# Deformable stages: transposes and hats first, pointwise sums in the taps' PSUM banks, first positions read one stage earlier

## What is computed

```python
def deform_block(x, ow, ob, dw, pw, pb, K):
    offsets = conv2d(x, ow, ob, K // 2)             # 2*K*K channels
    out = deform_depthwise(x, offsets, dw, K, K // 2)
    return conv2d(out, pw, pb, 0)                   # pointwise, 128 -> 128
...
# deform_depthwise: for each of K*K taps, sample x bilinearly at (gy+ky+dy, gx+kx+dx), times dw[tap], summed
out3 = deform_block(c3, ..., 3); out5 = deform_block(c5, ..., 5); out7 = deform_block(c7, ..., 7)
out = jnp.concatenate([out3, out5, out7], axis=1)
return out * se_weight(out, fc1_w, fc2_w)           # squeeze and excitation over mean and maximum
```

## Time and profile before

| | us |
|---|---|
| median of 3 runs (lowest, highest) | 7206.5 (7201.03, 7209.59) |
| the profiled execution, as timed | 7206.31 |
| its span, first to last instruction | 7204.5 |
| TensorE busy | 6456.0 (90%) |
| VectorE busy | 5057.3 (70%) |
| ScalarE busy | 4072.4 (57%) |
| GpSimd busy | 800.5 (11%) |
| mean granted TensorE clock, as a share of 2.4 GHz | 0.949 |

### The profile page before, as it was taken

One profiled execution on the slowest core, in us unless ns is written; L12 is line 12 of the kernel. 1 busy time (PEld: TensorE's weight loads), 2 busy tenths in 40 slices (PEclk: granted clock), 3 DMA queues, 4 the chain that ended last, 5 costly groups with the idle time before them and its releaser, 6 DMA issues. The chain is left out here.

```text
span 7204.5 us, 129062 instructions
## 1 busy us (share of the span) xinstructions
PE 6456.0 (90%) x48970; PEld 4356.8 (60%) x48970; DVE 5057.3 (70%) x10274; ACT 4072.4 (57%) x5674; POOL 800.5 (11%) x580
## 2 busy tenths in 40 slices
PE   6999999999998788998888988889888896999898
PEld 3555555555554455786557865578655785555598
DVE  6877877877877577887778877788777887233323
ACT  3655656656655255786557865578655785111132
POOL 3211211211211200201002010020100200000000
PEclk9999999999999899899998999989999898999899
DMA  3010000000000443554435544355443554010499
GB/s 114 16 33 24 16 33 24 16 33 24 17 33 20 118 114 90 130 116 112 110 91 133 115 113 108 85 136 118 115 100 89 132 122 123 27 44 35 108 224 207
DMA packets 182729, 616.12 MB, mean 86 GB/s; under 512 B 56553, under 2 KB 65185, under 8 KB 139347
## 3 DMA queue, kind: packets, MB, share of 16 engines
q1 hardware_dynamic: 182019, 606.89, 33.5%
HBM read 540.66 MB, written 65.59 MB: 84 GB/s over the span
## 5 line engine op out<-in xcount | busy, mean ns | idle before, releaser
L2288 PE MATMUL b_p<-m_S,b_hkt 64*128 64x144 f32 (+37 forms) x27520 | 2119.5, 309 | 300.1 <-DVE b_acc L2170 144.1
L2288 PEld LDWEIGHTS b_p<-m_S,b_hkt 64*128 64x128 f32 x27520 | 1970.2, 195 | 526.0 <-DVE m_S L2237 267.0
L2237 DVE TENSOR_TENSOR m_S<-m_rx,m_ry 128x140 f32<-128x140 f32 (+26 forms) x5312 | 1618.0, 357 | 359.2 <-PE b_p L2288 177.6
L2142 ACT ACTIVATE m_rx<-m_pp,b_mcol 128x512 f32<-128x512 f32 (+6 forms) x1328 | 764.9, 647 | 901.5 <-DVE m_S L2237 899.4
L539 ACT ACTIVATE a_ex<-a_p_t 128x1024 f32<-128x1024 f32 x526 | 539.0, 1025 | 719.1 <-PE a_p_t L471 717.1
L603 DVE TENSOR_REDUCE a_nm<-a_p_x 128x1 f16<-128x1024 f32 x537 | 658.3, 1226 | 279.1 <-PE a_p_x L460 262.0
L2146 ACT ACTIVATE m_ry<-m_pp,b_mrow 128x544 f32<-128x544 f32 (+6 forms) x1328 | 762.5, 645 | 0.0
L2170 DVE SCALAR_TENSOR_TENSOR b_acc<-b_p,b_dwc,b_acc 128x323 f32<-128x323 f32 (+14 forms) x1088 | 624.8, 577 | 189.9 <-PE b_p L2288 189.9
L1725 PE MATMUL b_p<-b_hp,b_ow 128*98 128x512 f32 x1568 | 732.4, 618 | 0.0
L609 DVE TENSOR_TENSOR a_el<-a_ex,a_eh 128x1024 f16<-128x1024 f32 x525 | 692.9, 1320 | 11.3 <-issue 7.7
L2178 DVE SCALAR_TENSOR_TENSOR b_acc<-b_p,b_dwc,b_acc 128x1024 f32<-128x1024 f32 x384 | 491.1, 1279 | 99.0 <-PE b_p L2288 97.6
(11 more groups left out here) (217 smaller groups left out, 6884.1 us busy)
## 6 DMA issues: line engine op xcount, KB each, us to landing
m_pp<-sampling_positions SPq DMA_DIRECT2D x664, 512.0 KB, 6.4
d_win<-merged_kernels SPq DMA_DIRECT2D x192, 263.0 KB, 6.8
b_xin<-x SPq DMA_DIRECT2D x24, 1024.0 KB, 8.4
a_xr<-in_x SPq DMA_DIRECT2D x12, 1536.0 KB, 6.4
a_xh<-in_x SPq DMA_DIRECT2D x9, 1536.0 KB, 6.4
x<-a_xr SPq DMA_DIRECT2D x9, 1536.0 KB, 5.8
c_xs<-x SPq DMA_DIRECT2D x9, 1536.0 KB, 6.3
b_xr<-x SPq DMA_DIRECT2D x13, 1024.0 KB, 14.1
```

Of the source, the lines that this page charges most:

```text
L2142: last = e.activation(rx[:, u, xo[c]:xo[c + 1]].rearrange("p (a b) -> p a b", a=H), pp[:, b, 1, :].rearrange("p (a b) -> p a b", a=H)[:, : ...
L2237: e.tensor_tensor(S[:, k % NS, 0:(r1 - r0) * w].rearrange("p (a b) -> p a b", b=w), rx[:, u, xo[cc]:xo[cc + 1]].rearrange("p (a b) -> p a ...
L2288: last = e.matmul(G[:, a0 - top:z0 - top, c0 - left:c1 - left], hkt[64 * s:64 * s + 64, SIDE * cr + cc, :], S[64 * s:64 * s + 64, k % NS, ...
```

## The change

- TensorE begins a stage with the transposes, and VectorE, not ScalarE, copies them to `hkt`. The four pointwise matmuls follow and write `ps[1]` and `ps[2]`, banks of the taps that the first part of tap 0 doesn't use, with no wait between them.
- ScalarE begins with the hats of tap 0, then evacuates the pointwise sums (`take_sums`), then goes on to tap 1. TensorE waits for these evacuations before the second and third part that it writes (j = 1, 2).
- SyncE reads the positions of a stage's tap 0 at the end of the stage in front, as soon as a ring slot is free, and waits there until they have landed; the slot is shifted by `RING_AT` so that it fits. For the first stage the setup block does it.
- For that the tiles `pp`, `rx`, `ry`, `S` and the setup's and `sample_far`'s tiles are cut from one room `work` that lives through the layer.

```diff
 FIRST_UNITS = 8
...
-        self.bank = [0, 1] * 4 + ([1] * SE_UNITS + [0] if g == 0 else [c % 2 for c in range(len(own))])
+        self.bank = [0, 1] * 2 + ([1] * SE_UNITS + [0] if g == 0 else [c % 2 for c in range(len(own))])
...
+        work = a.sb("work", [P, 16960])
+        pp, rx, ry, S = carve(work, [((NB, 2, N), F32), ((2, HAT), F32), ((2, HAT), F32), ((NS, WIDEST), F32)])
...
+        def read_positions(e, pp, g, tap, sem):
+            for s in range(2):
+                e.dma_start(pp[64 * s:64 * s + 64, (tap + RING_AT[g]) % NB, :, :], posd[g][s, 2 * tap:2 * tap + 2, :].partition_broadcast(64)).then_inc(sem.sem, 16)
...
+        def sums_in_taps(e, gp):
+
+            for i in range(4):
+                s, n = divmod(i, 2)
+                e.matmul(ps[1 + s][:, n, :], pw[:, gp, :], acc[:, s, n * HALF:(n + 1) * HALF], start=True, stop=True).then_inc(s_pw.sem, 1)
+
+        def take_sums(e, gp, stage):
+            for i in range(4):
+                s, n = divmod(i, 2)
+                e.wait_ge(s_pw.sem, s_pw.at(stage * 4 + i + 1))
+                e.sem_inc(sh["tick"], 1)
+                e.activation(dcv[:, gp, s, n * HALF:(n + 1) * HALF], ps[1 + s][:, n, :], ACT.Identity, bias=pb[:, gp:gp + 1],
+                             accum_out=sums[:, gp, s, n:n + 1]).then_inc(s_pe.sem, 1)
+
...
+                        for r in range(2):
+                            e.wait_ge(s_st[r].sem, s_st[r].at(FIRST_UNITS // 4 * 16))
+                        read_positions(e, pp, 0, 0, taps[0].s_pp[RING_AT[0]])
...
-                    pp = am.sb("pp", [P, NB, 2, N])
-                    rx = am.sb("rx", [P, 2, HAT])
-                    ry = am.sb("ry", [P, 2, HAT])
-                    S = am.sb("S", [P, NS, WIDEST])
...
-                            if tap < TAPS:
-                                b = tap % NB
+                            if 0 < tap < TAPS:
+                                b = (tap + RING_AT[g]) % NB
                                 if tap >= NB:
                                     e.wait_ge(tp.s_ab.sem, tp.s_ab.at(2 * (tap - NB + 1)))
-                                if tap == 1:
-                                    e.wait_ge(tp.s_pp[0].sem, tp.s_pp[0].at(32))
-                                for s in range(2):
-                                    e.dma_start(pp[64 * s:64 * s + 64, b, :, :], posd[g][s, 2 * tap:2 * tap + 2, :].partition_broadcast(64)).then_inc(tp.s_pp[b].sem, 16)
+                                read_positions(e, pp, g, tap, tp.s_pp[b])
                             if tap == 0 and g == 2:
...
+                        done = next(n for n in range(TAPS - NB, TAPS) if (n + RING_AT[g]) % NB == RING_AT[nxt])
+                        e.wait_ge(tp.s_ab.sem, tp.s_ab.at(2 * (done + 1)))
+                        ahead = taps[nxt].s_pp[RING_AT[nxt]]
+                        read_positions(e, pp, nxt, 0, ahead)
+                        e.wait_ge(ahead.sem, ahead.at(32))
...
-                        filled(e, us[7])
+                        filled(e, us[3])
...
-                        take_pointwise(e, gp, us[0:4])
-                        for j in range(4):
-                            u = us[4 + j]
-                            filled(e, u)
-                            part = bank_of(u[1]).rearrange("p (i c) -> p i c", c=P)
-                            e.activation(hkt[:, 4 * j:4 * j + 4, :], part, ACT.Copy, scale=-1.0 if j >= TURNED else 1.0).then_inc(s_cu[u[1]].sem, 1)
                         for tap in range(TAPS):
-                            u, b = tap % 2, tap % NB
+                            u, b = tap % 2, (tap + RING_AT[g]) % NB
                             (rows, yo), (cols, xo) = tap_spans(K, tap)
...
+                            if tap == 0:
+                                take_sums(e, gp, stage)
...
-                                    filled(e, us[3])
+                                    e.wait_ge(s_pw.sem, s_pw.at(stage * 4 + 4))
+                                    e.sem_inc(sh["tick"], 1)
...
-                                largest(e, gp, s, us)
+                                e.wait_ge(s_pe.sem, s_pe.at(stage * 4 + 2 * s + 2))
+                                e.sem_inc(sh["tick"], 1)
+                                largest(e, gp, s)
...
+                        for j in range(4):
+                            filled(e, us[j])
+                            part = bank_of(us[j][1]).rearrange("p (i c) -> p i c", c=P)
+                            e.tensor_scalar(hkt[:, 4 * j:4 * j + 4, :], part, -1.0 if j >= TURNED else 1.0, None, ALU.mult).then_inc(s_cu[us[j][1]].sem, 1)
                         if K in QUARTERED:
-                            filled(e, us[3])
+                            e.wait_ge(s_pw.sem, s_pw.at(stage * 4 + 4))
+                            e.sem_inc(sh["tick"], 1)
                             e.memset(acc[:], 0.0).then_inc(tp.s_g.sem, 1)
...
-                        pointwise(e, gp, us[0:4])
                         e.wait_ge(s_h8.sem, s_h8.at(pr * 3 + g + 1))
                         for j in range(4):
-                            free_bank(e, us[4 + j])
+                            free_bank(e, us[j])
                             for i in range(4):
-                                last = e.transpose(bank_of(us[4 + j][1])[:, i * P:(i + 1) * P], h8[:, 4 * j + i, :, :, :].rearrange("p s i j -> p (s i j)"), sh["ident"][:])
+                                last = e.transpose(bank_of(us[j][1])[:, i * P:(i + 1) * P], h8[:, 4 * j + i, :, :, :].rearrange("p s i j -> p (s i j)"), sh["ident"][:])
                             last.then_inc(s_pu.sem, 1)
+                        sums_in_taps(e, gp)
                         for c, k in plan.ahead:
                             convolve(c, k)
-                        for u in us[6:8]:
+                        for u in us[2:4]:
                             used(e, u)
                         for tap in range(TAPS):
...
+                                    if n not in begun and j in (1, 2):
+                                        e.wait_ge(s_pe.sem, s_pe.at(stage * 4 + 2 * j))
+                                        e.sem_inc(sh["tick"], 1)
```

More of the change, by code:

```diff
@@ L1 @@
+import math
 from contextlib import ExitStack
@@ L1261, in tap_spans, with carve @@
     return out
+def carve(room, sizes):
+    out, at = [], 0
+    for shape, dt in sizes:
+        n = math.prod(shape)
+        view = room[:] if dt == F32 else room[:].bitcast(dt)
+        per = 1 if dt == F32 else 2
+        names = "abcd"[:len(shape)]
+        view = view[:, at * per:at * per + n]
+        if len(shape) > 1:
+            view = view.rearrange(f"p ({' '.join(names)}) -> p {' '.join(names)}", **dict(zip(names, shape)))
+        out.append(view)
+        at += -(-n // per)
+    assert at <= room.shape[1], (at, room.shape)
+    return out
 HAT = max(tap_spans(K, tap)[axis][1][SIDE] for K in KS for tap in range(K * K) for axis in range(2))
@@ new lines, in sample_far @@
+    E, zero, hk, hi, stack, yk = carve(common["work"], [((2, ROWS * W), F16), ((HALF,), F16), ((2, CHUNKS, P), F32), ((N,), F16),
+                                                        ((NB, N), F16), ((NB, ITEMS, P), F32)])
+    bf = {**common, "E": E, "hk": hk, "hi": hi, "stack": stack, "y": yk, "NS": 5, "sum": ps[0:2], "p_r": [ps[2 + i // 2][:, i % 2, :] for i in range(4)],
+          "px": dcv, "wk": ow[:, 0:T7 // KS[-1] * P].rearrange("p (k c) -> p k c", c=P),
+          "py": ow[:, KS[-1] * P:KS[-1] * P + NB * N].rearrange("p (b n) -> p b n", b=NB),
+          "S": xin[:].rearrange("p s n -> p (s n)")[:, 0:15 * P].rearrange("p (i n) -> p i n", i=5)}
@@ new lines, in sample_far, with _ @@
+    clear(nc, [sem.sem for sem in s_far.values()])
+    with nc.Fori(0, 2 * FAR + 1) as f, nc.Fori(0, K) as ky:
+        with nc.Block() as block:
+            credit(sh, block, tfar)
+        with nc.Block() as block:
+            far_row(nc, sh, block, K, tfar, bf, ky, first + f * FAR_STEP - FAR * FAR_STEP)
+        clear(nc, [sem.sem for sem in tfar.all])
+    with nc.Block() as block:
+        @block.scalar
+        def _(e):
+            for s in range(2):
+                e.copy(acc[:, s, :], ps[s][:].rearrange("p a n -> p (a n)")).then_inc(s_far["ev"].sem, 1)
+            e.wait_ge(s_far["ev"].sem, s_far["ev"].at(2))
+        @block.sync
+        def _(e):
+            e.dma_start(dcv[:].rearrange("p g s n -> p (g s n)"), common["dcvd"]).then_inc(s_far["sp"].sem, 16)
+            e.dma_start(ow[:], common["owd"]).then_inc(s_far["ld"].sem, 16)
+            e.wait_ge(s_far["sp"].sem, s_far["sp"].at(16))
+            e.wait_ge(s_far["ld"].sem, s_far["ld"].at(16))
@@ L1630, in layer1 @@
+    clear(nc, [s_far[n].sem for n in ("ev", "sp", "ld")])
 def layer1(nc, sh, x, t, y):
@@ new lines, in clear_first, with stack_weights @@
+        def clear_first(e):
+            e.memset(ows[:], 0.0).then_inc(s_iv.sem, 1)
+            e.memset(hp[:], 0.0).then_inc(s_iv.sem, 1)
+            e.wait_ge(s_iv.sem, s_iv.at(2))
```

(14 more changed lines are left out.)

306 lines of the change are left out of this document (137 added, 169 removed).

## The result

The changed kernel takes 7142.8 us (median of 4 runs, 7138.7 to 7144.2); the kernel before, run beside it on the same chip, 7203.8 (7199.5 to 7209.6). The ratio is 0.9913 with a 95% interval of 0.9901 to 0.9924: faster by 0.87%, 61 us. The forecast was 7138. The profiled execution has a span of 7142.4 us against 7204.5, and a mean granted clock of 0.954 against 0.949.

What follows compares the result with a forecast made beforehand. TensorE bounds the bodies, a chain through ScalarE the heads of K = 3 and K = 7. Gains 6.9 + 3.0 + 7.6 - 0.5 = 17.0 us a pair, 68 for four: 7138 us, range 7112 to 7172 (8 in 10).

Steps and rivals of the forecast that it cites:

- large gain: Rival (7116 us, chance 0.12): whole clock loss recovered, VectorE's 6 us passed on in K = 5, ScalarE early.
- Transposes end at T+3.9, copies near 0.74 us, nothing between.: Stage head: 16 transposes end 3.9 us after TensorE's first instruction (T); VectorE's copies take 0.74 us each.
- K = 7, 7.6 us: Head of K = 7: ScalarE starts its hats earlier, so tap 1's hats end 7.6 us sooner.
- my chain: ScalarE in K = 7's head: start T-2.2, hats to T+5.4, evacuations to T+8.9, tap 1's hats to T+16.6.
- K = 3, 5.9 us for the head: Head of K = 3: sums, then memset, put the first product at T+9.9, 5.9 us earlier.
- the sums are done at T+7.5: Stage head: four fp32 matmuls at full clock, 3.6 us, end 7.5 us after TensorE's first instruction.
- K = 3, the clock at the first products: After a 2.4 us gap the granted clock stays up; worth up to 1.7 us, counted as 1.0.
- The late close of K = 3, 0.5 us (bounds 0 to 4.8): End of K = 3: the wait for position reads behind the 1 MB store costs 0.5 us.
- K = 5, 3.0 us: Head of K = 5: first product at T+13.9, 2.4 us earlier; with VectorE's lead 3.0, bounds 2.0 and 6.0.
- small gain: Rival (7174 us, chance 0.19): ScalarE arrives with TensorE or later, clock falls again, K = 3's reads land late.
- Slower: Rival (7228 us, chance 0.03): the block's end waits for positions, some 7.5 us a stage.
- no effect: Rival (7195 to 7206 us, chance 0.04): the head's lead is used up within the stage.

Runs made afterwards that it cites:

- experiment 1: The changed kernel with tap 0's positions read again in their own stage: 7180.1 us, ratio 0.9957 to the kernel before.
- experiment 2: The changed kernel with the four copies of the transposed source back on ScalarE, ahead of the hats: 7175.9 us, ratio 0.9954 to the kernel before.
- experiment 4: The kernel before with only tap 0's positions read in the stage in front; old order, banks and copies: 7203.0 us, ratio 0.9991.
- experiment 6: The changed kernel with the memset of acc moved to the twelfth item of tap 0: 7129.4 us, ratio 0.9896 to the kernel before.
- experiment 5: The changed kernel with the next stage's position reads issued ahead of K = 3's 1 MB result store: 7138.7 us, ratio 0.9909.
- experiment 8: The changed kernel with reads ahead of the store, late memset, and transposes 3 and 4 in ps[0]: 7118.1 us (ratio 0.9876), again 7130.2 (0.9886).

## Why the prediction was right, and where it wasn't

The time was 4.8 us above the forecast of 7138, the mechanism is the one that it named, and experiments 1, 2 and 4 bear it out. One case was added up wrongly: "large gain" has 8.5 us for K = 3, where its own terms, 5.9 for the head and 1.7 for the clock, make 7.6. The steps:

- **Transposes end at T+3.9, copies near 0.74 us, nothing between.** Right in K = 5 and K = 7 (T+3.9 and T+3.8 in the mean), and 0.69 us a copy. In K = 3 they end at T+4.2 in one profile and T+6.1 in the other.
- **K = 7, 7.6 us: the sum right, two terms not.** It measured 7.3 in one profile and 10.2 in the other. ScalarE began not at T-2.2 but at T-3.7 in the mean of the first profile, 1.0 us after VectorE's last instruction; TensorE took 4.4 us or more. By my chain that would have brought tap 1's hats to T+15.1 or, bound by the last sum, T+16.1; the mean is T+16.5. The second profile's 2.9 us more arise during the stage (the last tap's hats end at T+446.5 against T+449.5), not in its head; their cause is open.
- **K = 3, 5.9 us for the head: too much.** The first product came 4.7 us earlier in one profile, 2.9 in the other. The step that failed is "the sums are done at T+7.5", with two terms too small and one left out. The sums ended at T+8.5 and T+10.4. Of the 1.0 and 2.9 us too much, 0.3 and 2.2 are the transposes' end, where I had put no pause, and 0.7 in both profiles is the sums themselves, 4.3 us where I had taken full clock and 3.6; the gap behind them was 2.66 us where I had 2.4.
- **The pause in K = 3's transposes, which the prediction hadn't.** It stands behind the tenth or eleventh of the 16 transposes, in the middle of a unit, where the program has no wait. In the eleven profiles with the new order it is there in 32 of the 33 stages K = 3 of pairs 2 to 4, with 0.15 to 5.19 us, and in none of pair 1 or of K = 5 and K = 7. Each time a 16 KB packet of the queue q8, which the page calls "instruction", had ended 1.2 to 1.7 us before TensorE went on (at 3327.75, and on at 3329.18, in the case shown). So I read the pause as TensorE waiting for its own code; that q8 brings TensorE's code is argued from these times and not shown. It was 2.3 to 5.2 us long in the eight stages in which SyncE issued its first reads of positions 1.5 us or more before T, and at most 0.9 us in the others; that these reads hold the code up wasn't tried. The clock goes with it: from T+3.7 to T+7.4 it was 1.00 in pair 1, which has no pause, and 0.50 to 0.90 in the pairs behind it, 0.65 to 0.77 in the mean of a profile against 0.80 to 0.91 in the three with the old order (experiment 4 among them). K = 5, which begins with the same transposes and no pause, has 0.78 to 0.95 with the old order and 0.73 to 0.90 with the new, ranges that overlap.
- **K = 3, the clock at the first products: wrong in the level, right in the amount.** "The clock stays near 1.00" reasoned from the 1.55 us gap of K = 5; after 2.7 us it fell, in pair 2 to 0.50, and in the others to 0.54, 0.66 and 0.74 in the lower of two 3.5 us stretches from T+10. But it recovers sooner: from T+13.5 to T+17 and on to T+21 its mean is 0.72 and 0.93, where it was 0.50 and 0.50. From tap 4 to the last, each tap's hats end 6.0 us earlier, 4.7 of the head and 1.3 more, where I had counted 1.0. In experiment 6, without the gap, it is 1.00 in both.
- **The late close of K = 3, 0.5 us (bounds 0 to 4.8): mis-sized,** 1.4 us (VectorE's end to T from 4.4 to 5.9), and experiment 5 shows the reads behind the 1 MB store to be the cause. 6.0 - 1.4 is the stage's 4.6 us. In K = 7 the distance is 4.8 against 4.5.
- **K = 5, 3.0 us: too little.** It gave 4.8 and 4.0. The ends of the taps' hats in the two timelines, relative to T, show how: 3.0 us earlier up to tap 8, 4.1 from tap 9, 5.0 from tap 16 to the end. The first 3.0 are the head's. The rest arises at two places in the body; the kernel of experiment 4, whose head is the old one, gains 1.0 to 1.5 us there too. So it doesn't come from the head, and its cause is open.
- **What I had not thought of: 5.8 us given back behind layer 1.** The stretch from the last block of layer 1 to the end takes 1147.6 and 1145.5 us in the two profiles of before, and 1148.2 to 1163.3, 1153.7 in the mean, in the twelve of kernels with the room `work`, that of experiment 4 among them. Only a part lies in the depthwise convolutions at the end. From the same instruction of VectorE, the 496th from its last, to the end of the program it is 501.1 and 499.2 us before and 503.9 and 504.8 after. The DMA group of their weights (KB each, median us to landing), first of before, then of after:

```profile
d_win<-merged_kernels SPq DMA_DIRECT2D x192, 263.0 KB, 6.8
```

```profile
d_win<-merged_kernels SPq DMA_DIRECT2D x192, 263.0 KB, 7.0
```

The change doesn't touch this layer; only the addresses of tiles differ. But the kernels of experiments 5 and 8, with the same room, have 499.0 and 500.6 us there, as before the change, so addresses alone don't account for it. That they are the cause wasn't tried, and with two profiles of before against twelve the whole is an observation, no more.

So the closeness of the total is partly luck: 17.0 forecast against 16.7 and 16.9 a pair. It is made of one term too large in K = 3 (4.6 and 2.8 us where 6.9 less 0.5 were counted), one too small in K = 5, K = 7 near its term in one profile and above it in the other, and a loss of 1.5 us a pair behind the layer which the sum didn't hold. Of the rivals, "small gain" had the falling clock and the late reads right, and "large gain" ScalarE's arrival. "Slower" and "no effect" fell: the close waits 1.4 us, and the lead of the head is kept to the end of the stage (6.0 us at K = 3's tap 4 and at its last).

## What to carry to other kernels

When a head is a chain through several engines, ask of each part of an edit what the next link is without the others: here the read ahead brought next to nothing alone (ratio 0.9991) and 34.6 us with the new order. Move a job to the engine that has nothing queued behind it, even where it takes longer there (0.69 against 0.60 us, 30 us for the kernel). And let a clear wait until the first instruction that needs it, not until the earliest point at which it may run: it stood 1.76 us in front of everything. Last, look at the single stages and not only at their mean: the pause in K = 3's transposes took 0.3 us a stage in one profile of the changed kernel and 2.2 in the next.
